# Mamba scan and 3x3 convolutions on one core: how the convolution weights are made from the keys

## The reference, cut to what matters

```python
KSHAPE = (64, 64, 3, 3)
KSIZE = 64 * 64 * 9
w1 = (origin_weight[0:KSIZE] + jnp.einsum('i,if->f', new_param, P_weight[:, 0:KSIZE])).reshape(KSHAPE)
out = _conv3x3(x, w1, stride=1)
out = jax.nn.relu(_batchnorm(out, bn1_gamma, bn1_beta))
w2 = (new_param[39] * origin_weight[KSIZE:2 * KSIZE] + jnp.einsum('i,if->f', new_param, P_weight[:, KSIZE:2 * KSIZE])).reshape(KSHAPE)
out2 = _batchnorm(_conv3x3(out, w2, stride=1), bn2_gamma, bn2_beta)
```

## Time and profile before

| | |
|---|---|
| median of 3 runs | 28975.46 us (28960.53 to 28981.26) |
| profiled execution | 28998.67 us, of which the span of the profile is 28996.9 us |
| mean granted clock of the matrix engine | 0.759 of full speed |
| scan stage and norm stage, to the first DMA of the weight stage | 27076.5 us |
| weight stage, from the first key load's issue to the end of its last copy | 27077.87 to 27367.52 us |
| both convolutions and the end | from 27368.00 us on |

### The profile page before, as it was taken

One profiled execution on the slowest core, in us unless ns is written; L12 is line 12 of the kernel. 1 busy time (PEld: TensorE's weight loads), 2 busy tenths in 40 slices (PEclk: granted clock), 3 DMA queues, 4 the chain that ended last, 5 costly groups with the idle time before them and its releaser, 6 DMA issues. The chain is left out here.

```text
span 28996.9 us, 295604 instructions
## 1 busy us (share of the span) xinstructions
PE 19339.4 (67%) x63642; PEld 5895.2 (20%) x63642; DVE 26552.2 (92%) x29735; ACT 17085.9 (59%) x23617; POOL 24959.7 (86%) x10756
## 2 busy tenths in 40 slices
PE   6666666666666666666666666666666666662583
PEld 1111111111111111111111111111111111110441
DVE  8999999999999999999999999999999999996211
ACT  5666666666666666666666666666666666662032
POOL 8999999999999999999999999999999999993000
PEclk7777777777777777777777777777777777775596
DMA  5555555555555555555555555555555555558557
GB/s 184 193 196 197 194 194 195 193 193 194 194 193 195 193 196 196 195 195 196 194 194 193 196 198 195 196 195 194 195 197 196 196 194 194 195 196 187 108 121 178
DMA packets 1880801, 5506.97 MB, mean 190 GB/s; under 512 B 329944, under 2 KB 593896, under 8 KB 1865704
## 3 DMA queue, kind: packets, MB, share of 16 engines
q1 hardware_dynamic: 1878648, 5484.50, 55.4%
HBM read 4678.40 MB, written 805.31 MB: 189 GB/s over the span
## 5 line engine op out<-in xcount | busy, mean ns | idle before, releaser
L760 POOL TENSOR_TENSOR drive<-du_rep,b_rep 128x1024 f32<-128x1024 f32 x8192 | 19135.2, 2358 | 1397.4 <-DVE state L696 1148.4
L696 DVE TENSOR_TENSOR_SCAN decay<-decay,drive 128x512 f32<-128x512 f32 x11264 | 13129.8, 1211 | 334.5 <-ACT decay L572 172.4
L572 ACT ACTIVATE decay<-delta_rep,a_neg 128x1016 f32<-128x1016 f32 x8192 | 9044.0, 1108 | 2641.9 <-DVE state L696 1720.8
L709 DVE TENSOR_TENSOR read<-decay,c_rep 128x512 f32<-128x512 f32 x11264 | 7115.6, 671 | 0.0
L769 POOL TENSOR_TENSOR read<-state,c_rep 128x1024 f32<-128x1024 f32 x2560 | 6048.2, 2363 | 1.7 <-DVE state L696 1.7
L696 DVE TENSOR_TENSOR_SCAN state<-decay,drive 128x512 f32<-128x512 f32 x5120 | 5948.6, 1201 | 0.0
L435 PE MATMUL y_bank<-read,sel_f 128*32 128x512 f32 x32768 | 4924.1, 728 | 82.1 <-POOL read L769 57.7
L412 PE MATMUL p_bank<-e_one,sel_f 128*128 128x512 f32 x2048 | 1701.0, 925 | 3290.3 <-ACT e_one L555 1859.1
L399 PE MATMUL p_bank<-u,to_dt 128*128 128x512 f32 x2048 | 2119.6, 1138 | 2251.1 <-ACT zs L617 1408.7
L568 ACT COPY decay<-zeros 128x8 f32<-128x8 f32 x5632 | 932.1, 165 | 3773.9 <-DVE read L709 3761.7
L389 PE MATMUL p_bank<-xt,taps 128*128 128x512 f32 x4096 | 2816.3, 824 | 387.2 <-ACT bc L529 384.0
(11 more groups left out here) (89 smaller groups left out, 14397.2 us busy)
## 6 DMA issues: line engine op xcount, KB each, us to landing
du_rep<-du_spread SPq DMA_DIRECT2D x2048, 512.0 KB, 6.3
delta_rep<-delta_spread SPq DMA_DIRECT2D x2048, 512.0 KB, 8.3
b_rep<-bc_spread SPq DMA_DIRECT2D x2048, 512.0 KB, 8.4
c_rep<-bc_spread SPq DMA_DIRECT2D x2048, 512.0 KB, 7.6
du_spread<-e_log SPq DMA_DIRECT2D x512, 512.0 KB, 2.7
delta_spread<-e_one SPq DMA_DIRECT2D x512, 512.0 KB, 3.6
xt<-in_xs SPq DMA_DIRECT2D x1024, 128.0 KB, 3.5
bc_spread<-bc SPq DMA_DIRECT2D x1024, 64.0 KB, 2.0
```

The lines of the kernel that those rows point to most:

```text
L572: nc.scalar.activation(inner(place[:, :]), inner(delta_rep[:, j, :]), ACT.Exp, scale=a_neg[s][:, ROW * j + m:ROW * j + m + 1]).then_inc(s_ ...
L696: nc.vector.tensor_tensor_scan(out[:, px(d)][:, ::step], decay[PLACE[h][q]][:, px(d)][:, ::step], drive[:, q % DRIVE_RING, px(d)][:, ::ste ...
L709: nc.vector.tensor_tensor(read[:, q % READ_RING, px(d)], states[:, px(d)], c_rep[:, m, px(d)], ALU.mult).then_inc(s_read_v, 1)
L760: nc.gpsimd.tensor_tensor(drive[:, q % DRIVE_RING, :], du_rep[h][:, j, :], b_rep[:, m, :], ALU.mult).then_inc(s_drive, 1)
```

## The change

The operands of the matmul change places. `par` is spread by DVE to 32 equal columns (`spread`), and these 41x32 numbers become the stationary operand. The keys move past them, 512 flat weights at a time, and four calls with consecutive 512 flat weights go to the four column tiles of the array (tile positions (0, 0), (0, 32), (0, 64), (0, 96)), so that one PSUM bank takes 4 * 512 = 2048 flat weights (a "group"), each 512 of them repeated on 32 partitions. A convolution has 18 groups, in 3 chunks of 6 groups; a chunk is 12288 flat weights, 2.67 times the chunk before. ACT copies each bank to the tile `row[c]`.

As the weights now lie along rows and not by input channel, they go by way of DRAM. When all 18 groups of a convolution are copied, SP stores them to `flat` with four DMAs, one for each column tile, waits for these to land, and loads `raw[c]` (input channel on the partition) from `flat` twice, once for each half of the partitions; source and destination are then runs of 9 numbers. DVE turns (o, t) to (t, o) in one copy into w_conv. In the four stores the source is written as 32 partitions of 18 x 512 numbers and the destination as 18 x 512 numbers.

SP's order: the loads of chunks 0 to 4, then the layout of convolution 0, then the load of chunk 5, then the layout of convolution 1. The loads' rule is the same as before (chunk m when chunk m - 2 has been computed).

```diff
--- before.py
+++ after.py
@@ -945,14 +945,16 @@
             over_images(act, image)
 
 
-def weight_stage(nc, p_weight, origin, new_param, consts, w_conv):
-
-
-
-
-    CO = 8
-    CHUNK = CO * CH * KTAPS
-    CHUNKS = KSIZE // CHUNK
+def weight_stage(nc, p_weight, origin, new_param, consts, flat, w_conv):
+
+
+
+    GROUP = 4 * HALF
+    GROUPS = KSIZE // GROUP
+    CHUNKS = 3
+    PER = GROUPS // CHUNKS
+    WIDTH = PER * GROUP
+    BANKS = 4
     with ExitStack() as ctx:
         def sb(name, shape, dt=F32):
             return ctx.enter_context(nc.sbuf_tensor(name, shape, dt))
@@ -960,27 +962,21 @@
         def sem(name):
             return ctx.enter_context(nc.semaphore(name))
 
-        keys = [sb(f"w_keys{n}", [KEYS + 1, CHUNK]) for n in range(2)]
+        keys = [sb(f"w_keys{n}", [KEYS + 1, WIDTH]) for n in range(2)]
         par = sb("w_par", [KEYS + 1, 2])
-        raw = sb("w_raw", [P, 2 * CHUNKS, CO // 2, KTAPS])
-        made = [ctx.enter_context(nc.psum_tensor(f"w_made{n}", [P, HALF], F32)) for n in range(2)]
+        spread = sb("w_spread", [KEYS + 1, 2, 32])
+        row = [sb(f"w_row{c}", [P, GROUPS, HALF]) for c in range(2)]
+        raw = [sb(f"w_raw{c}", [P, CH, KTAPS]) for c in range(2)]
+        made = [ctx.enter_context(nc.psum_tensor(f"w_made{n}", [P, HALF], F32)) for n in range(BANKS)]
         s_par = sem("param_loaded")
+        s_spread = sem("param_spread")
         s_keys = [sem("keys_loaded0"), sem("keys_loaded1")]
         s_made = sem("weights_made")
-        s_raw = sem("weights_copied")
+        s_row = sem("weights_copied")
+        s_flat = sem("weights_stored")
+        s_raw = [sem("weights_by_channel0"), sem("weights_by_channel1")]
         s_laid = sem("weights_laid_out")
         block = ctx.enter_context(nc.Block())
-
-        def over_chunks(engine, chunk):
-
-            chunk(0, 0, 0)
-            chunk(1, 1, 0)
-            with engine.Fori(1, CHUNKS // 2) as i:
-                for n in range(2):
-                    chunk(2 * i + n, n, 0)
-            with engine.Fori(CHUNKS // 2, CHUNKS) as i:
-                for n in range(2):
-                    chunk(2 * i + n, n, 1)
 
         @block.sync
         def _(sp):
@@ -989,46 +985,61 @@
             sp.dma_start(par[KEYS:KEYS + 1, 0:1], consts[0:1, 2 * P:2 * P + 1]).then_inc(s_par, 16)
             sp.dma_start(par[KEYS:KEYS + 1, 1:2], new_param[KEYS - 1:KEYS, :]).then_inc(s_par, 16)
 
-            def chunk(m, n, c):
-                at_least(sp, s_made, m - 1)
-                at = bass.ds(m * CHUNK, CHUNK)
+            def load(m):
+                at_least(sp, s_made, PER * (m - 1))
+                n = m % 2
+                at = slice(m * WIDTH, (m + 1) * WIDTH)
                 sp.dma_start(keys[n][0:KEYS, :], p_weight[:, at]).then_inc(s_keys[n], 16)
                 sp.dma_start(keys[n][KEYS:KEYS + 1, :], origin[:, at]).then_inc(s_keys[n], 16)
-            over_chunks(sp, chunk)
+
+            def lay_out(c):
+                sp.wait_ge(s_row, GROUPS * (c + 1))
+                for j in range(4):
+                    sp.dma_start(flat[c:c + 1, :].rearrange("a (g j n) -> a j g n", j=4, n=HALF)[:, j],
+                                 row[c][32 * j:32 * j + 1, :, :]).then_inc(s_flat, 16)
+                sp.wait_ge(s_flat, 64 * (c + 1))
+                by_channel = flat[c:c + 1, :].rearrange("a (o i t) -> (a i) o t", i=CH, t=KTAPS)
+                for half in range(2):
+                    sp.dma_start(raw[c][64 * half:64 * half + 64, :, :], by_channel).then_inc(s_raw[c], 16)
+
+            for m in range(CHUNKS + 2):
+                load(m)
+            lay_out(0)
+            load(CHUNKS + 2)
+            lay_out(1)
 
         @block.tensor
         def _(pe):
-            pe.wait_ge(s_par, 64)
-
-            def chunk(m, n, c):
-                pe.wait_ge(s_keys[n], 16 * (m - n) + 32)
-                at_least(pe, s_raw, m - 1)
-                k = keys[n][:, :].rearrange("k (o q i t) -> k o t q i", q=2, i=CH, t=KTAPS)
-                for o in range(CO // 2):
-                    for t in range(KTAPS):
-                        col = o * KTAPS + t
-                        mm = nc.tensor.matmul(made[n][:, col:col + 1], k[:, o, t], par[:, c:c + 1],
-                                              start=True, stop=True)
+            pe.wait_ge(s_spread, 2)
+            for g in range(2 * GROUPS):
+                m = g // PER
+                if g % PER == 0:
+                    pe.wait_ge(s_keys[m % 2], 32 * (m // 2 + 1))
+                at_least(pe, s_row, g - BANKS + 1)
+                for j in range(4):
+                    at = (g % PER) * GROUP + j * HALF
+                    mm = nc.tensor.matmul(made[g % BANKS][32 * j:32 * j + 32, :], spread[:, g // GROUPS, :],
+                                          keys[m % 2][:, at:at + HALF], start=True, stop=True,
+                                          tile_position=(0, 32 * j), skip_group_check=True)
                 mm.then_inc(s_made, 1)
-            over_chunks(pe, chunk)
+
+        @block.scalar
+        def _(act):
+            for g in range(2 * GROUPS):
+                act.wait_ge(s_made, g + 1)
+                nc.scalar.copy(row[g // GROUPS][:, g % GROUPS, :], made[g % BANKS][:, :]).then_inc(s_row, 1)
 
         @block.vector
         def _(dve):
-            def chunk(m, n, c):
-                dve.wait_ge(s_made, m + 1)
-                nc.vector.tensor_copy(raw[:, bass.ds(m, 1), :, :].rearrange("p m o t -> p (m o t)"),
-                                      made[n][:, 0:CO // 2 * KTAPS]).then_inc(s_raw, 1)
-            over_chunks(dve, chunk)
-            dve.wait_ge(s_raw, 2 * CHUNKS)
+            dve.wait_ge(s_par, 64)
             for c in range(2):
-                for q in range(2):
-                    src = raw[64 * q:64 * q + 64, c * CHUNKS:(c + 1) * CHUNKS].rearrange(
-                        "p m o t -> p t (m o)")
-                    for half in range(2):
-                        dst = w_conv[c][64 * half:64 * half + 64, :, :].rearrange(
-                            "p t (o q) -> p t o q", q=2)[:, :, :, q]
-                        nc.vector.tensor_copy(dst, src).then_inc(s_laid, 1)
-            dve.wait_ge(s_laid, 8)
+                nc.vector.tensor_copy(spread[:, c, :], par[:, c:c + 1].broadcast_to([KEYS + 1, 32])
+                                      ).then_inc(s_spread, 1)
+            for c in range(2):
+                dve.wait_ge(s_raw[c], 32)
+                nc.vector.tensor_copy(w_conv[c][:, :, :], raw[c][:, :, :].rearrange("p o t -> p t o")
+                                      ).then_inc(s_laid, 1)
+            dve.wait_ge(s_laid, 2)
 
 
 def conv_stage(nc, tag, src, dst, w, affine, bn, consts, out_affine):
@@ -1289,6 +1300,7 @@
     x2 = nc.dram_tensor("x2", (BATCH, CH, SIDE * SIDE), F32, kind="Internal").ap()
     y1 = nc.dram_tensor("y1", (BATCH, CH, SIDE * SIDE), F32, kind="Internal").ap()
     y2 = nc.dram_tensor("y2", (BATCH, CH, SIDE * SIDE), F32, kind="Internal").ap()
+    flat = nc.dram_tensor("flat_weights", (2, KSIZE), F32, kind="Internal").ap()
     spill = {k: [nc.dram_tensor(f"{k}_spread{h}", (rows, WIDE), F32, kind="Internal").ap()
                  for h in range(2)] for k, rows in (("delta", P), ("du", P), ("bc", 2 * NS))}
     scan_stage(nc, a["xs"], rec, sets, a["select"], spill)
@@ -1296,7 +1308,7 @@
     with ExitStack() as ctx:
         w_conv = [ctx.enter_context(nc.sbuf_tensor(f"w_conv{c}", [P, KTAPS, CH], F32)) for c in range(2)]
         affine = [ctx.enter_context(nc.sbuf_tensor(f"affine{c}", [P, 2], F32)) for c in range(2)]
-        weight_stage(nc, a["p_weight"], a["origin"], a["new_param"], a["average"], w_conv)
+        weight_stage(nc, a["p_weight"], a["origin"], a["new_param"], a["average"], flat, w_conv)
         conv_stage(nc, "c1", x2, y1, w_conv[0], None, a["bn1"], a["average"], affine[0])
         conv_stage(nc, "c2", y1, y2, w_conv[1], affine[0], a["bn2"], a["average"], affine[1])
         end_stage(nc, y2, x2, out, affine[1])
```

## The result

| | before | after |
|---|---|---|
| median of 5 runs | 28973.32 us (28960.53 to 28981.26) | 28820.58 us (28818.42 to 28825.90) |
| ratio | | 0.9946 (95% interval 0.9936 to 0.9957) |
| profiled span | 28996.9 us | 28816.6 us |
| weight stage, first key load's issue to end of last layout copy | 289.65 us | 135.64 us |

The kernel is 152.7 us faster. The weight stage, read off the rows, is 154.0 us shorter: from 27048.72 to 27183.19 + 1.17 = 27184.36. The two profiled spans differ by 180.3 us. The other 26 us are no effect of the change: the stage starts 29.2 us earlier, after a scan and a norm stage that are the same in both, and what follows is 2.9 us longer. Such differences come and go between executions of one kernel: in a second trace of the changed kernel the stage started at 27068.60.

What follows compares the result with a forecast made beforehand. PE bounded the old weight stage, key loads the new: 85.2 + 24.3 + 1.7 + 12.2 + 16.7 = 140.1, then the tail, 192.2 us against 289.65, 97.5 less. Median forecast 28878 us, range 28809 to 28932.

Steps and rivals of the forecast that it cites:

- The likeliest case: Weight stage: 32 copies stored and small runs at 1.49 ns make it 192.2 us, kernel 28878 us; chance 0.47.
- rival 1: Weight stage's stores: only one copy is stored, hidden under load 4; stage 144.4 us, kernel 28830 us; chance 0.25.
- What bounds the stage before: Old weight stage: PE, 275.4 us of 289.65, at 0.239 us a pass, nearly all for 128 new stationary columns.
- PE's new work: Weight stage matmuls: four column tiles at once at 1.2 GHz, 10.2 us a chunk, 61 us for 36 groups.
- tiles take turns: PE in the weight stage: column tiles in strict turns, 6.8 us a group cold or 3.4 warm, 245 or 122 us.
- rival 3: PE in the weight stage: column tiles take turns at 1.2 GHz; stage 309 us, kernel 28995 us; chance 0.05.
- The loads: Key loads become the bound: 16.7 us a chunk at 121 GB/s, chunk 4 in SBUF at 85.2 us.
- The stores: Way by DRAM: 32 copies, 4.72 MB a convolution, 24.3 us each time, the first convolution's behind load 4.
- The small runs: Loads by channel: 8192 runs of 36 bytes a convolution, priced like 256-byte runs at 1.49 ns, 12.2 us.
- Rival 2: Loads by channel: 36-byte runs cost like 512 bytes, 3.0 ns; kernel 28902 us; 0.08 together with turns at 2.4 GHz.
- rival 4: Loads by channel: runs cost far more; at 15 ns each, stage 413 us, kernel 29099 us, slower; chance 0.08.
- The hole before load 5: SP's order: load 5, 16.7 us, is queued behind the DRAM round trip and small runs, ending at 140.1 us.

Runs made afterwards that it cites:

- the changed order: Load 5 issued before the layout of convolution 0 instead of behind it, against the changed kernel: weight stage 127.5 us, 8.2 less.

## Why the prediction was right or wrong

The range and the sign held, with 28820.6 us against 28878 forecast: 152.7 us less, not 97.5. The likeliest case was the wrong one. What happened is rival 1, which gave 145.3 us less and 28830, and had 0.25. The range holds because its low end, 28809, was set by rival 1 with the cheapest runs; the path that was thought likeliest does not lead there.

- **What bounds the stage before**: right. The experiments add that the price is the columns', with a small surcharge for their stride.
- **PE's new work**: right, 62.8 us busy against 61, a chunk 10.46 against 10.2. But the forecast kept "tiles take turns" as a rival because "no row of this trace has four tiles on the same rows". That is false. The scan's line 435 calls four column tiles (0, 0) to (0, 96) with all 128 rows, and the trace of the kernel before has it, here by order of time:

```profile
15005.86 1.92 PE L435 MATMUL y_bank<-read,sel_f 128*32 128x512 f32 x16
```

  16 passes in 1.92 us are 0.120 each, at a granted clock of 1.00. By the prediction's own price for strict turns at 2.4 GHz, 3.4 us for 8 passes, they would take 6.8. Read with the code, this row speaks against tiles in turn before any run. In rival 3's sum the 22 us for the first chunk come from no row: its own terms give 1.7 + 16.7 = 18.4, and 19.5 were measured without column tiles (27107.82 - 27088.29).
- **The loads**: right. 121 GB/s was taken, 126 measured; chunk 4 was put in SBUF at 85.2 us and PE began on it at 27133.16 - 27048.72 = 84.4. The reason given, the few destination partitions, outlived two rivals, but the number of DMAs in flight was not set apart from it.
- **The stores**: this is the step that failed. It charged 24.3 us twice for 32 copies, 48.6 us in all, where the diff stores one. Of the price, the last stores' 26.0 us were measured as 25.25. The first ones', set behind load 4, came out at 15.2, since they overlap with that load. So what failed is the reading of one slice; and had there been 32 copies, this term would still have been 9 us too long, for taking the stores to wait behind load 4. The first convolution's store did vanish under load 4, as rival 1 says: the loads by channel are issued at 27133.86, 0.7 us after PE starts on chunk 4. The second one's round trip took 6.16 us, not 2.5: the issue alone of four stores, 18 pieces from one partition each, takes 2.96 us.
- **The small runs**: the mechanism was right, the size was not. 1.49 ns a run was taken from 256-byte runs; 36-byte runs take 0.61. If a run cost 1.49 ns whatever its size, 36-byte runs would have cost it too; so the lower bound of 1.7 us by bytes was nearer than the 12.2 chosen, though 5.0 is three times it. That is 2 x 7.2 = 14.4 us too much. Rival 2 and rival 4, built on dearer runs, are out. The rule of the Trainium skill (DMA: Bandwidth & Descriptors, Specifications) on transfers under 512 bytes had backed rival 2; here 8192 runs of 36 bytes in 5.0 us are 59 GB/s, so line rate is indeed lost, but a run costs a fifth of the 3.0 ns that rival 2 had worked out. The measurement decides.
- **The hole before load 5**: seen and priced in the sum, and shown by the changed order to be worth 8.2 us.

With one copy and the measured runs, the same sum is 144.4 - 14.4 + 3.7 (the second round trip) = 133.7 us, against 135.6 measured. Most of the rest is at the end: from the issue of the last loads by channel to DVE's copy 8.37 us, where the sum has 1.7 + 5.0. Rival 1 came so near partly because its dear runs and its cheap round trip stand on opposite sides.

## What to carry to other kernels

Where a product has one moving column, swap the operands, but only with column tiles: 32 equal columns on one tile left PE at 245.9 us, four tiles made it 62.8. When such a change moves the bound to the loads, try destinations on both halves of the partitions and more loads in flight; cutting the rows of one load differently gave nothing here. Don't let SP wait for a round trip between two loads that another engine needs. And read a slice in a diff twice before pricing it: the largest error here was no property of the chip.

## What was not expected of the hardware

PE's clock stayed at 0.50 (1.2 GHz) with tile 0 alone (read from 27110 to 27360 in that trace), through 246 us in which PE was busy without a gap, each pass with 512 moving columns. It was 0.50 as well through the 275 us of the kernel before. The first convolution, with four tiles of 64x64 and the same 512 columns, reached 1.00 (2.4 GHz) within about 7 us of its first pass. In the changed kernel the stretch from PE's first chunk to its last is at 0.50 throughout. Why the clock rose in one and not in the others was not tried. For this kernel it matters little, since loads bound the stage: by an estimate from the chunk's 10.46 us, at 2.4 GHz only the last chunk's pass would shorten the stage, by about 5 us.

Small runs were cheaper than thought, 0.61 ns each for 36 bytes. And loads onto 41 partitions ran at 119 to 143 GB/s however their rows were cut or placed in DRAM, while onto twice 41, with more DMAs in flight, they ran at 163 to 201.
